# Moving six batches of the shared FFN into the scan loop, C's rows in two half buffers, and the row scaling to VectorE

## The chip, the cores and the metric

The kernel runs on one core of a Trainium2 chip. Time is the device time of one execution in microseconds (us). Before the change three runs took 1523.89, 1524.09 and 1526.13 us; the median is 1524.09.

## What is computed

x has 8 batches of 512 tokens with 256 channels, all in fp32. A layer norm, a selective scan (Mamba-like, 512 inner channels, 16 states), a residual with a norm, then a mixture of experts with a shared expert and one routed expert of eight per token:

```
h = silu(conv4(layernorm(layernorm(x)) @ in_proj_w.T))
dt_in, B, C = split(h @ x_proj_w.T);  dt = softplus(dt_in @ dt_proj_w.T + dt_proj_b)
state_t = exp(-exp(A_log) * dt_t) * state_(t-1) + B_t * h_t          # 512 x 16 values
y_t = sum_n(state_t * C_t) + D * h_t;   a = silu(y) @ out_proj_w.T + shortcut
x1 = x + layernorm(a);  xn = layernorm(x1)
shared = (silu(xn @ sh_gate) * (xn @ sh_up)) @ sh_down               # 256 -> 512 -> 256
e = argmax(xn @ gate_w);  xs = xn * sigmoid(max(xn @ gate_w))
out = x1 + layernorm(shared + (silu(xs @ rt_gate[e]) * (xs @ rt_up[e])) @ rt_down[e])
```

## The kernel before

**The scan loop.** A turn i of the loop handles the scans of batch i in 32 steps q: two halves of the 512 channels, 16 states each. At a step VectorE scans (L1067), ScalarE writes the decays of two steps ahead into PSUM (two exps, L711), and GpSimd weighs the state with C's row (L495). TensorE sums the weighed states into bank psY by 16 small matmuls in the profile (`total`, L1434). The scan's input is B's row times the channels: for even q GpSimd makes it (`inject`, L484) from rows that a DMA has spread over all partitions; for odd q TensorE spreads the row into bank psB by a matmul with a column of the identity (`spread_b`, L1426) and VectorE multiplies (L1055). In the same 32 steps run the front of batch i+1 (transposes L1340, in-projection L1350, taps L1007, dt row L1357, B and C rows L1363, softplus, dt sums L1377 to L1379) and the back of batch i-1 (out-projection L1393, norms, transposes L1407, expert logits L1416). Both share bank psF. Each engine's order is written out by the step q, and an engine runs strictly in it; a wait holds all that stands behind.

**Which waits matter here.** `spread_b` of step q+2 is issued at odd step q, after VectorE has consumed the bank at step q. `total(q-3)` waits for GpSimd's weighing. `decays(q+2)` waits for scan q. VectorE's L1030 waits for the out-projection. C's 16 rows of a batch lie in cbc, loaded once a turn in four groups of four (`load_c`), and serve both halves. SP issues nearly all loads and stores, each behind the waits before it.

**Behind the scans.** When the last batch's back is done, TensorE runs the shared FFN of all eight batches (L1490, L1512), each batch's columns xnT being loaded again from DRAM. Meanwhile VectorE works out the slots of the tokens, SP loads two batches of rows (xrow) and the routed weights (12.6 MB), GpSimd scales the rows by the score and scatters them, 4 indirect DMAs a batch (L550); the rows of batch b wait for the scatters of batch b-2. When all are scattered, SP loads slot tiles (L427), and TensorE runs 39 routed tiles (L1534, L1543, L1552, L1560). Then each token's result is gathered (L561), summed, normed and stored.

## Time and profile before

| | us |
|---|---|
| median of 3 runs | 1524.09 (1523.89 to 1526.13) |
| profiled execution | 1533.3, its span 1531.4 |
| turns 2 to 6 of the scan loop, each | 119.0 to 120.7 |
| turn 7 | 104.0 |
| shared FFN, first matmul to last | 1048.67 to 1218.4 |
| routed tiles | 1218.4 to 1466 |

The page says: TensorE busy 1204.2 us of the span, VectorE 1020.5, GpSimd 1014.7, ScalarE 799.8. A share of the whole says little here, because the stretches have different limits: GpSimd is busy nearly all of the scan loop and not at all in the routed stretch. The chain that ended last is laid on GpSimd for 36% of the span and on TensorE for 34%.

### The profile page before, as it was taken

The page shows a single profiled execution, that of the slowest core. Times are in us where ns is not written, and L with a number is a line of the kernel's source. Part 1 is how long each engine was busy: PE and PEld are TensorE (multiplying, and loading weights), DVE is VectorE, ACT ScalarE, POOL GpSimd, SP SyncE. Part 2 cuts the span into 40 slices and gives each one's busy share as a digit, 9 for nine tenths or more (in the row PEclk, how much of TensorE's full clock was granted, in tenths as well). Part 3 has the DMA queues.
Part 4 walks back from the last instruction along what each step waited for, and adds up shares of the span by engine and source line. Part 5 has one row for each costly group of instructions (what it writes and reads, how often), then busy time and mean ns, then how long its engine had stood idle before and what let it go on. Part 6 is the DMA issues. An engine that isn't in the chain of part 4 may idle for free.

```text
span 1531.4 us, 15602 instructions
## 1 busy us (share of the span) xinstructions
PE 1204.2 (79%) x4766; PEld 526.9 (34%) x4767; DVE 1020.5 (67%) x1059; ACT 799.8 (52%) x1386; POOL 1014.7 (66%) x476
## 2 busy tenths in 40 slices
PE   4774877869769878878887877757999999999920
PEld 2221223224224223223222322233655655665510
DVE  4698998998898998998998997924111022232245
ACT  6666667668658667668667664533111111111135
POOL 0599999999999999999999999931450000000043
PEclk9897899899899899899899898877999999999965
DMA  2802301401321220230230230027730111111144
GB/s 60 312 0 76 119 0 57 157 22 57 104 76 46 94 97 23 89 124 2 96 125 2 97 124 1 28 82 262 287 131 14 46 54 41 41 41 48 34 139 146
DMA packets 77953, 128.46 MB, mean 84 GB/s; under 512 B 7616, under 2 KB 56384, under 8 KB 73792
## 3 DMA queue, kind: packets, MB, share of 16 engines
q1 hardware_dynamic: 67120, 108.93, 20.6%
q10 hardware_dynamic: 7696, 10.36, 1.9%
q0 software_dynamic: 3072, 8.39, 1.7%
q8 instruction: 30, 0.49, 0.1%
q14 instruction: 35, 0.29, 0.1%
HBM read 95.94 MB, written 31.72 MB: 83 GB/s over the span
## 4 chain that ended last, share of the span: by engine, by line
POOL 36%; PE 34%; issue 13%; DVE 9%; ACT 7%; DMA 1%; another core or an unknown queue 0%; ACTq 0%; POOLq 0%; DVEq 0%
POOL state L495 22%; POOL bx L484 12%; PE psX L1543 10%; PE psX L1490 7%; DVE state L1067 4%; PE bank L1560 2%; PE psY L1560 2%; PE psY L1512 2%; PE bank L1512 2%; PE bank L1393 2%; PE psY L1434 1%; POOL lt L500 1%; DVE acc L1007 1%; ACT psX L711 1%; PE bank L1426 1%
## 5 line engine op out<-in xcount | busy, mean ns | idle before, releaser
L495 POOL TENSOR_TENSOR state<-state,cbc 128x1024 f32<-128x1024 f32 x256 | 606.4, 2391 | 12.5 <-DVE state L1067 12.4
L1067 DVE TENSOR_TENSOR_SCAN state<-psX,bx 128x1024 f32<-128x1024 f32 x256 | 578.0, 2278 | 42.9 <-ACT psX L711 23.9
L711 ACT ACTIVATE psX<-dt,aneg 128x511 f32<-128x511 f32 x512 | 330.6, 679 | 216.5 <-DVE state L1067 215.4
L484 POOL TENSOR_TENSOR bx<-xh,bbc 128x1024 f32<-128x1024 f32 x128 | 309.7, 2420 | 59.0 <-DMA bbc<-bc_rows 42.5
L1434 PE MATMUL psY<-state,ident 64*64 64x512 f32 x2048 | 303.2, 683 | 51.5 <-POOL state L495 51.3
L561 POOL DMA_INDIRECT fy<-slot_out,slot x32 | 31.9, 998 | 346.8 <-DMA slot_out<-yo 334.0
L1426 PE MATMUL bank<-prow,ident 128*128 128x512 f32 x256 | 170.2, 752 | 104.4 <-DVE bx L1055 104.2
L1055 DVE TENSOR_TENSOR bx<-xh,bank 128x1024 f32<-128x1024 f32 x128 | 152.9, 1194 | 0.5 <-PE bank L1426 0.5
L1434 PEld LDWEIGHTS psY<-state,ident 64*64 64x64 f32 x2048 | 64.8, 144 | 247.8 <-issue 123.7
L1221 DVE TENSOR_TENSOR actN<-sg,psX 128x512 f32<-128x512 f32 x39 | 26.8, 687 | 144.9 <-ACT sg L910 144.9
L1426 PEld LDWEIGHTS bank<-prow,ident 128*128 128x128 f32 x256 | 47.3, 220 | 202.2 <-DVE bx L1055 160.8
L910 ACT ACTIVATE sg<-psX 128x512 f32<-128x512 f32 x39 | 23.3, 597 | 161.6 <-PE psX L1543 161.6
L1174 DVE TENSOR_TENSOR actS<-sg,psX 128x512 f32<-128x512 f32 x32 | 21.9, 686 | 124.4 <-ACT sg L873 107.1
L1543 PE MATMUL psX<-wg,xsT 128*128 x156 | 78.8, 628 | 2.5 <-DVE xsT L1215 0.9
L1543 PE MATMUL psX<-wu,xsT 128*128 x156 | 73.9, 596 | 0.0
L1350 PE MATMUL bank<-lt,win 128*128 128x512 f32 x112 | 55.5, 618 | 20.7 <-DVE acc L1007 19.9
L1393 PE MATMUL bank<-wout,yv 128*128 128x256 f32 x256 | 61.5, 395 | 8.9 <-ACT yv L670 7.9
L873 ACT ACTIVATE sg<-psX 128x512 f32<-128x512 f32 x32 | 19.1, 597 | 92.2 <-PE psX L1490 92.2
L1007 DVE SCALAR_TENSOR_TENSOR acc<-bank,cw,acc 128x511 f32<-128x511 f32 (+2 forms) x84 | 62.3, 742 | 3.7 <-ACT acc L615 1.4
L1490 PE MATMUL psX<-xg,shg 128*128 128x512 f32 x128 | 62.1, 608 | 1.7 <-DVE actS L1174 1.7
L1490 PE MATMUL psX<-xg,shu 128*128 128x512 f32 x128 | 60.3, 593 | 0.0
L1393 PEld LDWEIGHTS bank<-wout,yv 128*128 128x128 f32 x256 | 48.7, 195 | 28.6 <-issue 12.7
(183 smaller groups left out, 1529.1 us busy)
## 6 DMA issues: line engine op xcount, KB each, us to landing
cbc<-bc_rows SPq DMA_DIRECT2D x32, 1024.0 KB, 5.1
bbc<-bc_rows SPq DMA_DIRECT2D x16, 1024.0 KB, 6.0
slot_in<-ao SPq DMA_DIRECT2D x1, 4992.0 KB, 27.3
xsl<-slot_in SPq DMA_DIRECT2D x39, 128.0 KB, 2.2
slot_out<-yo ACTq DMA_DIRECT2D x39, 128.0 KB, 2.4
xin<-in_x SPq DMA_DIRECT2D x8, 512.0 KB, 4.2
xr<-in_x SPq DMA_DIRECT2D x8, 512.0 KB, 5.8
x_rows<-ao SPq DMA_DIRECT2D x8, 512.0 KB, 2.9
```

Source lines behind the costliest of these rows:

```text
L484: nc.gpsimd.tensor_tensor(bx[q % RB][:], xh[par][:, h * CH:(h + 1) * CH], bbc[:, n // 2].unsqueeze(1).broadcast_to([P, CH, L]), ALU.mult). ...
L495: nc.gpsimd.tensor_tensor(w[:], w[:], cbc[:, n].unsqueeze(1).broadcast_to([P, CH, L]), ALU.mult).then_inc(weighted, 1)
L711: e = nc.scalar.activation(decay[q % RD][:, c, 1:L], dt[par][:, h * CH + c, 1:L], ACT.Exp, scale=aneg[:, h * CH + c, n:n + 1])
L1007: last = nc.vector.scalar_tensor_tensor(out=acc[:, c, m:L], in0=psF[:, 0:L - m], scalar=cw[:, c, TAPS - 1 - m:TAPS - m], in1=acc[:, c, m:L ...
L1055: nc.vector.tensor_tensor(bx[q % RB][:], xh[par][:, h * CH:(h + 1) * CH], psB[:].unsqueeze(1).broadcast_to([P, CH, L]), ALU.mult).then_inc ...
L1067: nc.vector.tensor_tensor_scan(st[q % RS][:].rearrange("p c t -> p (c t)"), decay[q % RD].rearrange("p c t -> p (c t)"), bx[q % RB][:].rea ...
L1393: last = nc.tensor.matmul(psF[:, (j % 2) * DIM:(j % 2 + 1) * DIM], yv[:, c, j * P:(j + 1) * P], wout[:, c], start=(c == 0), stop=(c == C - 1))
L1426: nc.tensor.matmul(psB[:], ident[:, n:n + 1].broadcast_to([P, P]), prow[par][:], start=True, stop=True).then_inc(b_bcast, 1)
L1434: done = nc.tensor.matmul(psY[o * HP:(o + 1) * HP, r], weights(half, c), src[half, c], start=first, stop=last_)
L1490: last = nc.tensor.matmul(bank, w[:, k, c * P:(c + 1) * P], xg[i][:, k], start=(k == 0), stop=(k == KC - 1))
L1512: last = nc.tensor.matmul((psF, psG)[j // 2][:, (j % 2) * DIM:(j % 2 + 1) * DIM], actS[gp][:, c, j * P:(j + 1) * P], shd[:, c], start=(c = ...
L1543: last = nc.tensor.matmul(bank, xsT[i][:, k], w[:, bass.ds(ereg[i], 1), k].rearrange("p a n -> p (a n)"), start=(k == 0), stop=(k == KC - 1))
```

## The change

**In the scan loop.** From turn 2 on, turn i also runs the shared FFN of batch i-2 (e below), whose columns xnTb are still in SBUF. It uses psB, the bank of the spread rows. At steps 1, 3, 5, 7 TensorE makes a quarter of the gate product, ScalarE copies it to `sga`, and applies Silu to all at step 10. At 13, 15, 17, 19 it makes a quarter of the up product, and VectorE multiplies it into `sga` from the bank. At 21, 23, 25, 27 it makes 128 tokens of the down product, and ScalarE copies them to `ystage`, which SP stores to DRAM. At these steps `spread_b(q+2)` is not issued; it is issued at q+1, as `spread_b(q+1)` in that step's terms, after a wait that the piece has been taken out of the bank. Other steps keep their order.

**To make room** C's rows are held in two slots of four rows, loaded in eight groups a turn. The shared weights are loaded at the start and stay.

**Behind the scans** TensorE runs the shared FFN of batches 6 and 7 only. The rows of all eight batches are loaded at once into the places of fx0 and ysh, VectorE scales them between its FFN products, and GpSimd only scatters. The stored shared rows of batches 0 to 5 (3 MB) are loaded behind x1's first half, before the third slot tile is asked for.

```diff
+    EARLY_AT = (1, 3, 5, 7, 13, 15, 17, 19, 21, 23, 25, 27)
+    CS = N // CG
+    LATE = 2
+    EARLY = NB - LATE
-        cbc = sb("cbc", [P, N, L], where=A)
+        cbc = sb("cbc", [P, 2 * CG, L], where=A)
+        sga = sb("sga", [P, FC, L], where=A)
+        ystage = sb("ystage", [P, J, DIM], where=A)
-        xrow = [sb(f"xrow{i}", [P, J, DIM], where=R) for i in range(2)]
+        xrow = [(fx0, ysh)[b // (NB // 2)][:, b % (NB // 2) * J:(b % (NB // 2) + 1) * J] for b in range(NB)]
 # SP
+            for dst, src in ((shg, sh_gate), (shu, sh_up), (shd, sh_down)):
+                sp.dma_start(dst[:], src.rearrange("(k p) n -> p k n", p=P)).then_inc(sh_loaded, 16)
+            def load_c(f, k):
+                g, slot = k % CS, k % 2
+                if not (isinstance(f, int) and f == 0 and k < 2):
+                    sp.wait_ge(weighted, Q * f + CG * (k - 1))
...
+                if do_scan and not (isinstance(i, int) and i < 2):
+                    e = i - 2
+                    sp.wait_ge(e_kept, J * (e + 1))
+                    sp.dma_start(pick(yshb_v, e), ystage[:]).then_inc(e_stored, 16)
                 if do_front:
-                    load_b(f, 1 - par, 1)
+                    load_c(f, 0)
...
-            sp.wait_ge(s_down, 2 * NB)
             load_residual(fx0, 0)
+            sp.wait_ge(e_stored, 16 * EARLY)
+            sp.dma_start(ysh[:, 0:EARLY * J, :], ysht_v[:, 0:EARLY * J, :]).then_inc(ysh_loaded, 16)
 # GpSimd
-                pool.wait_ge(xrow_loaded[b % 2], 16 * (b // 2 + 1))
-                nc.gpsimd.tensor_tensor(xrow[b % 2][:], xrow[b % 2][:],
-                                        score[:, b * J:(b + 1) * J].unsqueeze(2).broadcast_to([P, J, DIM]),
-                                        ALU.mult).then_inc(xrow_scaled, 1)
                 pool.wait_ge(xrow_scaled, b + 1)
 # ScalarE
+            def early(e, q):
+                if q in (1, 3, 5, 7):
+                    c = q // 2
+                    act.wait_ge(e_gate, FC * e + c + 1)
+                    nc.scalar.activation(sga[:, c], psB[:], ACT.Identity).then_inc(e_gate_kept, 1)
+                if q == 10:
+                    act.wait_ge(e_gate_kept, FC * (e + 1))
+                    nc.scalar.activation(sga[:], sga[:], ACT.Silu).then_inc(e_silu, 1)
+                if q in (21, 23, 25, 27):
+                    j = (q - 21) // 2
+                    act.wait_ge(e_down, J * e + j + 1)
...
+                    nc.scalar.activation(ystage[:, j], psB[:, 0:DIM], ACT.Identity).then_inc(e_kept, 1)
 # VectorE
+            def early_act(e, c):
+                dve.wait_ge(e_silu, e + 1)
+                dve.wait_ge(e_up, FC * e + c + 1)
+                nc.vector.tensor_tensor(sga[:, c], psB[:], sga[:, c], ALU.mult).then_inc(e_act, 1)
...
+                    if do_choose and q in (13, 15, 17, 19):
+                        early_act(i - 2, (q - 13) // 2)
...
+            scale_rows(0)
+            for u in range(2, LATE * FC):
+                scale_rows(u - 1)
                 sh_act(u // FC, u // FC, u % FC)
...
+            scale_rows(NB - 1)
 # TensorE
+            def early(e, q):
+                if q in (1, 3, 5, 7, 13, 15, 17, 19):
...
+                    for k in range(KC):
+                        last = nc.tensor.matmul(psB[:], w[:, k, c * P:(c + 1) * P], xnTb[:, k],
+                                                start=(k == 0), stop=(k == KC - 1))
+                    last.then_inc(e_gate if gate else e_up, 1)
+                if q in (21, 23, 25, 27):
...
+                        last = nc.tensor.matmul(psB[:, 0:DIM], sga[:, c, j * P:(j + 1) * P], shd[:, c],
+                                                start=(c == 0), stop=(c == FC - 1))
...
+            def early_taken(e, q):
+                if q in (1, 3, 5, 7):
+                    pe.wait_ge(e_gate_kept, FC * e + q // 2 + 1)
+                if q in (13, 15, 17, 19):
+                    pe.wait_ge(e_act, FC * e + (q - 13) // 2 + 1)
+                if q in (21, 23, 25, 27):
+                    pe.wait_ge(e_kept, J * e + (q - 21) // 2 + 1)
...
                 for q in range(Q):
-                    if q % 2 == 1:
+                    if do_scan and i >= 2:
+                        if q in EARLY_AT:
+                            pe.wait_ge(dve_bx, i * DQ + q // 2 + 1)
+                            early(i - 2, q)
+                        if q - 1 in EARLY_AT:
+                            early_taken(i - 2, q - 1)
+                            spread_b(i, par, q + 1)
+                    if q % 2 == 1 and not (do_scan and i >= 2 and q in EARLY_AT):
```

TensorE's order in a turn of the loop, from step 13 to the first half of the out-projection of step 15, first in the kernel before. `bank<-prow` is a spread into psB, `psY<-state` a total, `bank<-xh,w_bc` the B and C rows, `bank<-wout,yv` half of the out-projection.

```order
L1426 MATMUL bank<-prow,ident 128x512
L1434 MATMUL psY<-state,ident 64x512 x8
L1363 MATMUL bank<-xh,w_bc 128x512 x4
L1426 MATMUL bank<-prow,ident 128x512
L1434 MATMUL psY<-state,ident 64x512 x4
L1393 MATMUL bank<-wout,yv 128x256 x8
```

The same place after the change; `bank<-xnTb,shu` is an up product.

```order
L1470 MATMUL bank<-xnTb,shu 128x512 x2
L1494 MATMUL psY<-state,ident 64x512 x4
L1456 MATMUL bank<-prow,ident 128x512
L1494 MATMUL psY<-state,ident 64x512 x4
L1393 MATMUL bank<-xh,w_bc 128x512 x4
L1470 MATMUL bank<-xnTb,shu 128x512 x2
L1494 MATMUL psY<-state,ident 64x512 x4
L1423 MATMUL bank<-wout,yv 128x256 x8
L1456 MATMUL bank<-prow,ident 128x512
```

Two up products have come in, at the head of steps 13 and 15. The spread that stood at the head of step 15, ahead of the out-projection, stands behind it now.

TensorE's order at steps 25 to 28, before: L1377 to L1379 are the three matmuls that sum dt for a quarter of the channels.

```order
L1426 MATMUL bank<-prow,ident 128x512
L1434 MATMUL psY<-state,ident 64x512 x4
L1377 MATMUL bank<-acc,ident 128x512
L1378 MATMUL bank<-tmp,ident 128x512
L1379 MATMUL bank<-lt,minus 128x512
L1434 MATMUL psY<-state,ident 64x512 x4
L1377 MATMUL bank<-acc,ident 128x512
L1378 MATMUL bank<-tmp,ident 128x512
L1379 MATMUL bank<-lt,minus 128x512
L1426 MATMUL bank<-prow,ident 128x512
```

And after, from the spread of the same row on, which stood ahead of the dt sums of step 25 and stands behind them now, at step 26; `bank<-shd,sga` is a down product.

```order
L1456 MATMUL bank<-prow,ident 128x512
L1494 MATMUL psY<-state,ident 64x512 x4
L1407 MATMUL bank<-acc,ident 128x512
L1408 MATMUL bank<-tmp,ident 128x512
L1409 MATMUL bank<-lt,minus 128x512
L1477 MATMUL bank<-shd,sga 128x256 x4
L1494 MATMUL psY<-state,ident 64x512 x4
L1407 MATMUL bank<-acc,ident 128x512
L1408 MATMUL bank<-tmp,ident 128x512
L1409 MATMUL bank<-lt,minus 128x512
L1456 MATMUL bank<-prow,ident 128x512
```

The down product of step 27 stands between the dt sums of steps 26 and 27, and the last spread, which stood ahead of the dt sums of step 27, stands behind them.

ScalarE's order at the end of step 26 and at step 27, before: half an application of the norm to xr, a pair of exps, the copy of dt, the other half.

```order
L592 ACTIVATE xr<-ao,nmr,rstd 128x256 x2
L707 REGISTER_ALU
L711 ACTIVATE psX<-dt,aneg 128x511 x2
L655 ACTIVATE dt<-bank 128x512
L592 ACTIVATE xr<-ao,nmr,rstd 128x256 x2
```

And after:

```order
L610 ACTIVATE xr<-ao,nmr,rstd 128x256 x2
L740 REGISTER_ALU
L744 ACTIVATE psX<-dt,aneg 128x511 x2
L673 ACTIVATE dt<-bank 128x512
L610 ACTIVATE xr<-ao,nmr,rstd 128x256 x2
L727 ACTIVATE ystage<-bank 128x256
```

The copy out of psB (`ystage<-bank`) is the last thing of step 27.

## Rows read from the trace of the kernel before

**Rows 1.** busy time by stretch: length, busy us by engine, granted clock, DMA share, GB/s

```profile
545.50:665.60 120.10, 97.51 (x432) 34.51 (x424) 109.26 (x95) 86.25 (x143) 117.78 (x51) 0.90 0.22 78
...
903.70:1007.70 104.00, 75.87 (x347) 22.59 (x346) 85.90 (x66) 52.03 (x96) 104.00 (x46) 0.82 0.07 26
1048.67:1218.40 169.73, 167.99 (x517) 98.61 (x517) 31.23 (x64) 29.57 (x49) 47.44 (x46) 0.99 0.41 147
```

**Rows 2.** order of time, GpSimd, one turn: start us, us, what, waits

```profile
582.99 2.35 POOL L495 TENSOR_TENSOR state<-state,cbc 128x1024 f32<-128x1024 f32 x1 [0.34 <-DVE state L1067]
...
612.87 2.37 POOL L495 TENSOR_TENSOR state<-state,cbc 128x1024 f32<-128x1024 f32 x1 [1.57 <-DVE state L1067]
```

**Rows 3.** order of time, VectorE, the same turn

```profile
586.89 4.47 DVE L1067 TENSOR_TENSOR_SCAN state<-psX,bx 128x1024 f32<-128x1024 f32 x2 [0.69 <-ACT psX L711]
...
597.05 1.20 DVE L1055 TENSOR_TENSOR bx<-xh,bank 128x1024 f32<-128x1024 f32 x1
601.32 0.69 DVE L1030 TENSOR_TENSOR ao<-bank,ao 128x512 f32<-128x512 f32 x1 [3.07 <-PE bank L1393]
...
614.89 1.20 DVE L1055 TENSOR_TENSOR bx<-xh,bank 128x1024 f32<-128x1024 f32 x1
...
629.86 1.19 DVE L1055 TENSOR_TENSOR bx<-xh,bank 128x1024 f32<-128x1024 f32 x1
...
645.12 1.20 DVE L1055 TENSOR_TENSOR bx<-xh,bank 128x1024 f32<-128x1024 f32 x1
...
656.67 2.29 DVE L1067 TENSOR_TENSOR_SCAN state<-psX,bx 128x1024 f32<-128x1024 f32 x1 [1.25 <-ACT psX L711]
```

**Rows 4.** order of time, TensorE, the same turn

```profile
567.75 1.98 PE L1350 MATMUL bank<-lt,win 128*128 128x512 f32 x4 [1.69 <-DVE acc L1007]
...
579.06 2.07 PE L1426 MATMUL bank<-prow,ident 128*128 128x512 f32 x2 [5.00 <-DVE bx L1055]
...
592.05 3.70 PE L1363 MATMUL bank<-xh,w_bc 128*128 128x512 f32 x8 [0.60 <-ACT acc L626]
595.59 1.02 PE L1426 MATMUL bank<-prow,ident 128*128 128x512 f32 x2
...
597.56 3.72 PE L1393 MATMUL bank<-wout,yv 128*128 128x256 f32 x16
...
635.02 1.53 PE L1377 MATMUL bank<-acc,ident 128*128 128x512 f32 x2
```

**Rows 5.** order of time, ScalarE, the same turn

```profile
565.52 1.30 ACT L711 ACTIVATE psX<-dt,aneg 128x511 f32<-128x511 f32 x2 [1.69 <-DVE state L1067]
566.76 2.06 ACT L592 ACTIVATE ao<-xr,nmr,rstd 128x256 f32<-128x256 f32 x4
...
580.54 1.91 ACT L621 ACTIVATE xh<-acc 128x2048 f32<-128x2048 f32 x1
...
638.31 0.60 ACT L655 ACTIVATE dt<-bank 128x512 f32<-128x512 f32 x1 [1.44 <-PE bank L1379]
```

**Rows 6.** DMA issues by line: count, KB each, median us to landing

```profile
cbc<-bc_rows SPq DMA_DIRECT2D x32, 1024.0 KB, 5.1
```

**Rows 7.** order of time behind the scans: GpSimd, SP's queue

```profile
1136.60 0.96 POOL L550 DMA_INDIRECT slot_in<-xrow,slot  x1 [0.30 <-issue]
...
1139.06 0.82 SPq L427 DMA_DIRECT2D xsl<-slot_in  x2
```

**Rows 8.** groups by line, gathers and scatters: count | busy us, mean ns

```profile
L561 POOL DMA_INDIRECT fy<-slot_out,slot x32 | 31.9, 998 | 346.8 <-DMA slot_out<-yo 334.0 <-issue 9.1 <-remote 3.7
L550 POOL DMA_INDIRECT slot_in<-xrow,slot x32 | 31.3, 977 | 9.5 <-issue 7.3 <-POOL xrow L544 2.2
```

**Rows 9.** busy time by stretch while the routed weights load

```profile
1080.00:1090.00 10.00, 10.00 (x41) 7.50 (x40) 0.69 (x1) 1.79 (x3) 0.00 (x0) 1.00 1.06 401
```

**Rows 10.** order of time, TensorE, start of the routed stretch

```profile
1218.43 0.38 PE L1534 MATMUL bank<-ident,xsl 128*128 128x128 f32 x2
...
1227.35 0.66 PE L1534 MATMUL bank<-ident,xsl 128*128 128x128 f32 x2 [3.17 <-issue]
```

More of the change, by code:

```diff
@@ L151, in build @@
         actS = [sb(f"actS{i}", [P, FC, L], where=MS) for i in range(2)]
+        xg = [sb(f"xg{i}", [P, KC, L], where=MS) for i in range(2)]
         MS.close()
@@ L271, in build @@
         ex_ready = sem("ex_ready")
-        xrow_loaded = [sem(f"xrow_loaded{i}") for i in range(2)]
+        xrow_loaded = [sem(f"xrow_loaded{i}") for i in range(NB)]
         xrow_scaled = sem("xrow_scaled")
@@ L369, in iteration @@
                 if do_scan:
-                    load_c(i, par, 3)
+                    for k in range(1, 5):
+                        load_c(i, k)
                 if do_front:
@@ L1516, in sh_down_ @@
                         last.then_inc(s_down, 1)
[L1518 removed]
+            for u in range(2, LATE * FC):
                 sh_up_(u // FC, u % FC, u // FC)
             sh_down_(0, 0)
[L1521 to L1526 removed]
+            sh_down_(1, 1)
             def xsT_(s, i):
```

139 lines of the change are left out of this document (68 added, 71 removed).

## The prediction

> **What bounds the kernel now.** I read the busy times by stretch first. One turn of the scan loop (32 steps q, the scans of one batch) takes 119 to 121 us, and GpSimd is busy for 117.8 us of a turn of 120.1, VectorE for 109.3, TensorE for 97.5, ScalarE for 86.3 [rows 1]. The last turn, with no front of a next batch, takes 104.0. Then come two stretches bound by TensorE: the shared FFN (busy 168.0 of 169.7 us) and the routed one [rows 1]. So in the scans GpSimd sets the pace, but how far VectorE runs ahead of it decides what an addition elsewhere costs. GpSimd's order of time shows it: at steps 11 and 19 of a turn it starts within 0.1 us of VectorE's scan, after waits of 0.34 and 1.57 us [rows 2, 3]. The next turn's scan 0 ends at 658.96 and is weighed at 665.60 [rows 1, 3]: 6.6 us of lead, gone again by step 11. A delay of VectorE between steps 11 and 19 is therefore paid in full, and one between 20 and 31 is paid at the next step 11. VectorE waits 3.07 us at step 16 for the output projection [rows 3], and there TensorE works without a gap: from 592.05 on its rows touch until the projection's second half is done, 607.96 [rows 4]. It has idle time elsewhere (5.00 us before step 11's spread), and 0.90 is its mean granted clock in that turn [rows 1, 4].
>
> **The shared FFN among the scans (six turns, 2 to 7).** Each turn gains 12 pieces in bank psB: 4 gate products at steps 1 to 7, 4 up products at 13 to 19, 4 down products at 21 to 27. A gate or up product is shaped like the in-projection (1.98 us as a row, 1.82 from its start to the next one's), a down product is half of an L1393 row of 3.65, so 1.8: 12 x 1.8 = 22 us for TensorE. VectorE gains 4 products like the additions of 0.69 us, of which 0.62 counts back to back: 2.5 us. ScalarE gains 4 copies of 0.60, 4 of half that size, and one Silu of 1.91 [rows 3 to 5]. That alone would fit. What does not fit is the bank: the spread of row q+2 was issued two steps ahead; now it waits at step q+1 until the piece has been taken out, and who takes it out is an engine in order. I walk through the turn, "late" meaning against the rows.
>
> Gates. After scan q ScalarE does two exps (1.30), then the copy (0.60), then TensorE spreads (1.1): 3.0 us, while VectorE needs 2.2 for scan q+1. At 3, 5 and 7 the three taps (2.2) cover this, but at 5 and 7 ScalarE has moments or a 2.06 us application ahead of the copy: together 1.2 us late. At step 1 the gate product stands ahead of the transposes of the next front, and their copy ahead of its own: 2.3 us. Sum 3.6 [rows 4, 5].
>
> Ups. The Silu at step 10 stands ahead of exps 13, for which VectorE already waits (0.69 before 586.89): 1.8 late at scan 13. The row of L1363 starts 1.9 late, at 593.9, since z comes later. Behind it now stand an up product and a total before the projection, which ends at 604.0 where 601.2 was. The spread for step 17, which stood ahead of the projection (595.59), now stands behind it: inject 17 at 605.05 where it was 597.05, scan 17 at 606.9 where it was 601.9 (601.32 and the 0.61 of the addition), some 4.9 late. The next up product and again a spread behind the projection give scan 19 6.9 late, and inject 21 at 622.6 for 614.89: 7.7 late [rows 3, 4].
>
> Downs. At 21 the copy waits behind an application: 1.7, of which the end of VectorE's wait for GpSimd's `loss` gives back nearly all. At 23 it stands behind Relu and half an application: inject 25 at 640.0 for 629.86, 10.1 late. From step 25 to 28 TensorE has no gap (in the old turn its rows touch from 635.02 on), so the pieces of 25 and 27 lengthen it by 3.6, and the piece of 27 leaves the bank only after the copy of dt, which follows its three matmuls, and half an application (1.0): inject 29 at 661.9 for 645.12, 16.7 late. VectorE's old waits for ScalarE there (the longer is 1.25, before 656.67) give back 1.4: 15.3 at the next scan 0. If the wait of 4.6 us before the spread of 25 lets the clock fall to its lower level, as 5.00 us of idle did before 579.06 (the spread took 2.07 there instead of 1.1), 1.2 to 2 more [rows 3 to 5].
>
> A turn grows by 3.6 + 15.3 + 1.7 = 20.6 us; five turns (2 to 6) by 103. The ends are far apart: VectorE's 2.5 us and its present waits alone give 5, all 22 us of TensorE with the bank's round trips 28. I take 20.6, the walk, since the waits it adds hang on rows with names. In turn 7 there is no front: VectorE needs 112 for its walk with twelve waits of 0.8 where GpSimd needs 104 after a start 9.9 us behind: 114 against 113.9 from scan 0 on, nothing.
>
> **C's rows by halves.** Eight loads a turn for four, 5.1 us each from issue to landing [rows 6]; a load is let go when its slot's group is done and is wanted four steps (14 us) later. SP issues in order, and ahead of group 0 of the next turn stand the stores of xn and of the shared rows, which wait for ScalarE's step 27; that leaves some 9 us. I take 0, with GpSimd's own waits as the cover; if it goes, up to 5 us a turn. The three shared weights are loaded at the start behind wout, 1.5 MB in an idle queue: 0.
>
> **The stretch behind the scans.** Six of eight batches leave the shared FFN, so TensorE is free at about 1097. Then the scatter is the end of the wait. Before, GpSimd scattered batches 0 and 1 at once, then waited for its rows behind the routed weights, and scaled each batch itself; the last of 32 went at 1136.60 and SP asked for the first slots at 1139.06 [rows 7]. Now all rows are in place and VectorE scales. VectorE's first scaling comes behind its routing (1066.2), so the first scatter is 1 us later, at 1067.5; then 32 x (0.98 + 0.30) = 41 us [rows 8], the last at 1107, slots asked for at 1109.6. The weights saturate the queues at 401 GB/s [rows 9], 17 MB from 1049 with 3 MB more rows ahead of them: in at about 1101, not the end. The first slot transpose, at 1218.43 before [rows 10], comes at 1112. There a wait grows: the third slot load stood behind 2 MB of x1 (TensorE waits 3.17 us, until 1227.35 [rows 10]); now also behind 3 MB of stored shared rows, 8 us at the same rate: until 1127.5. Gain 1227.35 - 1127.5 = 99.9, less 1 to 2 for a clock that falls in the longer wait: 98. Bounds: 92 if the scatter's landings lag, 104 if the 3 MB are quick. The 39 routed tiles and the end are unchanged.
>
> Here a rule can be weighed. VectorE now scales with both inputs in SBUF while GpSimd issues scatters. In the trace 32 gathers with VectorE's additions beside them took a mean of 998 ns, 32 scatters without them 977 [rows 8]: 0.7 us in all, which the sum leaves out. The Trainium skill (SBUF — State Buffer, Who interferes with whom) says that a VectorE instruction with two SBUF inputs takes the read port that GpSimd shares and holds it for the whole instruction, and infers that descriptor writing is spared. By the hold alone eight scalings would cost up to 8 x 1.2 = 10 us; by the inference nothing, and the trace agrees with the inference.
>
> **Sum.** 103 + 0 - 98 = +5. The profiled execution took 1533.3 us (span 1531.4); the median of the runs is 1524.1, so I put +6 on it, rounding up for clock falls: 1530.
>
> **Rivals.** (1) The waits overlap: VectorE, once late, finds ScalarE's and TensorE's queues empty, and a turn grows by 12 only. For it speaks that TensorE idles 22 us a turn [rows 1]; against it that the additions sit where it does not. 5 x 12 - 98 = -38: 1486. Chance 0.27. (2) GpSimd stays the bound, the lead of 6.6 us takes the additions, a turn grows by 3: 15 - 98: 1441. Against it rows 2: no lead at steps 11 to 19. 0.08. (3) The lower clock level meets the pieces too, in the stretches behind each new wait: a turn grows by 26: 1558. 0.15. (4) C's halves come late, 5 us a turn on top: 1555 and above, deciding once a load takes over 14 us from its release. 0.05. (5) The forecast, a turn of 136 to 145: 0.45.
>
> **How the numbers follow.** A measurement of this kernel tells 0.2%, 3 us, from no change. The forecast's case spreads 15 us to each side: of its 0.45, 0.28 is slower, 0.10 the same, 0.07 faster. Faster: 0.27 + 0.08 + 0.07 = 0.42; same 0.10; slower 0.28 + 0.15 + 0.05 = 0.48. The forecast's own range is 1512 to 1550. The range for 8 in 10 takes in most of rivals 1, 3 and 4 and leaves out rival 2: 1482 to 1560.
>
> **What would show it.** In the profile after: turns of 136 to 145 us by the distance of GpSimd's first weighings; GpSimd busy about 85% of one, waiting for the scan; VectorE's inject waiting for the bank, most at steps 17, 19, 25 and 29; the first slot transpose some 106 us earlier relative to the last weighing than the 210.7 us of before, and about 10 us of idle TensorE before the third. Turns under 130 us, or GpSimd waits put down to a DMA of cbc, would prove the walk wrong.

## The result, and the profile after

The changed kernel took 1541.6 us (median of 4 runs, 1539.33 to 1541.9) where the kernel before took 1525.07 in the same series (4 runs, 1523.89 to 1526.13): a ratio of 1.0105 (1.0088 to 1.0123). In a second series it was 1542.64 against 1522.46, 1.0126 (1.0105 to 1.0148). So it is slower by 1.1 to 1.3%, 16 us in the first series and 20 in the second, where 6 were forecast. The profiled execution took 1541.9 us, its span 1540.2.

I cut both spans at the same places of the work (us; the scans' and weighings' starts and ends, TensorE's third slot transpose, the first gather):

| stretch | before | after | difference | forecast |
|---|---|---|---|---|
| scan 0 of turn 2 to scan 0 of turn 7 | 596.5 | 706.7 | +110.2 | +103 |
| scan 0 of turn 7 to the last weighing's end | 113.9 | 120.7 | +6.8 | 0 |
| from there to the third slot transpose | 219.7 | 122.2 | -97.5 | -98 |
| routed tiles, up to the first gather | 244.2 | 240.7 | -3.5 | 0 |
| first gather to the end of the span | 59.8 | 52.6 | -7.2 | 0 |

Ahead of the first row both take 297 us. The last row is most likely not the change's: the experiment before_again and its neighbours speak for that below. Without it the sum is +16, which is what the ratio of the first series says.

Busy time by stretch, after: a turn of the loop twice, then the last weighings of turn 7.

```profile
440.10:582.10 142.00, 116.29 (x488) 44.73 (x488) 114.19 (x100) 92.77 (x154) 118.32 (x51) 0.95 0.29 100
582.10:725.30 143.20, 119.52 (x488) 46.06 (x488) 113.68 (x99) 91.12 (x151) 118.21 (x50) 0.93 0.28 96
1007.10:1124.70 117.60, 91.13 (x430) 33.77 (x430) 95.25 (x74) 60.78 (x111) 106.62 (x46) 0.94 0.23 87
```

GpSimd's work in a turn is what it was (118.2 us against 117.78 [rows 1]), but the turn is 22 us longer, so its share falls to 83% (118.21 of 143.2): it is no longer the bound. No other engine is the new one either: TensorE is busy for 119.5 of 143.2, VectorE for 113.7. What fills the turn are waits, and the costliest groups and the chain of waits of the page say whose:

```profile
PE 47%; DVE 18%; ACT 16%; issue 9%; POOL 7%; DMA 1%; ACTq 0%; DVEq 0%; POOLq 0%; SPq 0%
...
L518 POOL TENSOR_TENSOR state<-state,cbc 128x1024 f32<-128x1024 f32 x256 | 606.7, 2384 | 67.1 <-DVE state L1088 66.6
...
L1456 PE MATMUL bank<-prow,ident 128*128 128x512 f32 x256 | 157.3, 699 | 147.2 <-DVE bx L1076 57.5
L1076 DVE TENSOR_TENSOR bx<-xh,bank 128x1024 f32<-128x1024 f32 x128 | 154.3, 1205 | 117.1 <-PE bank L1456 117.0
```

GpSimd was 36% of the chain and is 7%. It waits 66.6 us for VectorE's scans (L1088) before its weighings and another 74.9 before its own injects (L506). VectorE's inject (L1076) waits 117.0 us for the spread (L1456): in turns 3 to 6 these waits of VectorE are 33 and take 79.1 us, where the kernel before had none. The spread in turn is held by the piece that is in the bank.

### The profile page after: what moved, and what is told of

It is laid out like the page before. It is cut to its first block, busy times and chain, and to the rows that moved or that the text cites. A ratio compares the mean times of both kernels' runs of the same rounds, so it can differ in the third digit from the quotient of the medians.

```text
span 1540.2 us, 15716 instructions
## 1 busy us (share of the span) xinstructions
PE 1199.0 (78%) x4766; PEld 518.9 (34%) x4767; DVE 1036.7 (67%) x1067; ACT 812.1 (53%) x1404; POOL 1007.4 (65%) x468
## 4 chain that ended last, share of the span: by engine, by line
PE 47%; DVE 18%; ACT 16%; issue 9%; POOL 7%; DMA 1%; ACTq 0%; DVEq 0%; POOLq 0%; SPq 0%
DVE state L1088 10%; PE psX L1604 10%; PE psY L1494 6%; PE bank L1456 5%; ACT psX L744 4%; PE bank L1423 4%; DVE bx L1076 3%; PE bank L1470 3%; PE bank L1621 2%; PE bank L1380 2%; POOL slot_in L568 2%; PE psY L1621 2%; PE bank L1407 2%; POOL state L518 2%; POOL fy L579 2%
## 5 line engine op out<-in xcount | busy, mean ns | idle before, releaser
L518 POOL TENSOR_TENSOR state<-state,cbc 128x1024 f32<-128x1024 f32 x256 | 606.7, 2384 | 67.1 <-DVE state L1088 66.6
L1088 DVE TENSOR_TENSOR_SCAN state<-psX,bx 128x1024 f32<-128x1024 f32 x256 | 579.3, 2279 | 41.1 <-ACT psX L744 25.1
L506 POOL TENSOR_TENSOR bx<-xh,bbc 128x1024 f32<-128x1024 f32 x128 | 308.6, 2411 | 118.0 <-DVE state L1088 74.9
L1494 PE MATMUL psY<-state,ident 64*64 64x512 f32 x2048 | 295.9, 662 | 11.0 <-POOL state L518 11.0
L1456 PE MATMUL bank<-prow,ident 128*128 128x512 f32 x256 | 157.3, 699 | 147.2 <-DVE bx L1076 57.5
L1076 DVE TENSOR_TENSOR bx<-xh,bank 128x1024 f32<-128x1024 f32 x128 | 154.3, 1205 | 117.1 <-PE bank L1456 117.0
L1494 PEld LDWEIGHTS psY<-state,ident 64*64 64x64 f32 x2048 | 61.1, 139 | 197.2 <-issue 149.9
L926 ACT ACTIVATE sg<-psX 128x512 f32<-128x512 f32 x39 | 23.3, 597 | 184.7 <-PE psX L1604 184.7
L1456 PEld LDWEIGHTS bank<-prow,ident 128*128 128x128 f32 x256 | 43.8, 203 | 227.4 <-DVE bx L1076 79.8
L1023 DVE SCALAR_TENSOR_TENSOR acc<-bank,cw,acc 128x511 f32<-128x511 f32 (+2 forms) x84 | 62.5, 745 | 7.6 <-ACT acc L633 5.4
L1244 DVE COPY xsT<-bank 128x256 f32<-128x256 f32 x39 | 16.5, 424 | 62.4 <-PE bank L1595 62.4
L1477 PE MATMUL bank<-shd,sga 128*128 128x256 f32 x192 | 52.1, 418 | 7.5 <-DVE bx L1076 7.5
L1470 PE MATMUL bank<-xnTb,shu 128*128 128x512 f32 x96 | 48.5, 629 | 7.3 <-DVE bx L1076 7.3
L1470 PE MATMUL bank<-xnTb,shg 128*128 128x512 f32 x96 | 49.3, 639 | 2.1 <-DVE bx L1076 2.1
```

Of the source, the lines that this page charges most:

```text
L506: nc.gpsimd.tensor_tensor(bx[q % RB][:], xh[par][:, h * CH:(h + 1) * CH], bbc[:, n // 2].unsqueeze(1).broadcast_to([P, CH, L]), ALU.mult). ...
L518: nc.gpsimd.tensor_tensor(w[:], w[:], cbc[:, n % (2 * CG)].unsqueeze(1).broadcast_to([P, CH, L]), ALU.mult).then_inc(weighted, 1)
L1076: nc.vector.tensor_tensor(bx[q % RB][:], xh[par][:, h * CH:(h + 1) * CH], psB[:].unsqueeze(1).broadcast_to([P, CH, L]), ALU.mult).then_inc ...
L1088: nc.vector.tensor_tensor_scan(st[q % RS][:].rearrange("p c t -> p (c t)"), decay[q % RD].rearrange("p c t -> p (c t)"), bx[q % RB][:].rea ...
L1456: nc.tensor.matmul(psB[:], ident[:, n:n + 1].broadcast_to([P, P]), prow[par][:], start=True, stop=True).then_inc(b_bcast, 1)
L1470: last = nc.tensor.matmul(psB[:], w[:, k, c * P:(c + 1) * P], xnTb[:, k], start=(k == 0), stop=(k == KC - 1))
```

## How a turn grew

VectorE's waits for the spread in turn 4 that are longer than 1.7 us. Scan 0 of the turn starts at 579.42 (before at 537.2, so that 42.2 is to be added to the times of [rows 2 to 5] to compare):

```profile
590.71 1.22 DVE L1076 TENSOR_TENSOR bx<-xh,bank 128x1024 f32<-128x1024 f32 x1 [3.21 <-PE bank L1456]
...
653.42 1.22 DVE L1076 TENSOR_TENSOR bx<-xh,bank 128x1024 f32<-128x1024 f32 x1 [2.64 <-PE bank L1456]
...
662.25 1.22 DVE L1076 TENSOR_TENSOR bx<-xh,bank 128x1024 f32<-128x1024 f32 x1 [2.03 <-PE bank L1456]
...
688.90 1.22 DVE L1076 TENSOR_TENSOR bx<-xh,bank 128x1024 f32<-128x1024 f32 x1 [3.19 <-PE bank L1456]
...
712.19 1.22 DVE L1076 TENSOR_TENSOR bx<-xh,bank 128x1024 f32<-128x1024 f32 x1 [6.48 <-PE bank L1456]
```

These are the injects of steps 3, 17, 19, 25 and 29: the four that the prediction named, and step 3, to which it gave less. (At step 23 it waits 1.65 us, at 7 and 9 some 0.3.) TensorE at steps 15 to 17 and 24 to 29; a total (L1494) is 8 small matmuls in the profile, not 16:

```profile
645.98 1.88 PE L1470 MATMUL bank<-xnTb,shu 128*128 128x512 f32 x4
647.79 1.09 PE L1494 MATMUL psY<-state,ident 64*64 64x512 f32 x8
648.81 3.72 PE L1423 MATMUL bank<-wout,yv 128*128 128x256 f32 x16
652.37 1.02 PE L1456 MATMUL bank<-prow,ident 128*128 128x512 f32 x2
...
686.79 2.08 PE L1456 MATMUL bank<-prow,ident 128*128 128x512 f32 x2 [4.20 <-ACT ystage L727]
688.79 1.99 PE L1494 MATMUL psY<-state,ident 64*64 64x512 f32 x8
690.71 3.19 PE L1477 MATMUL bank<-shd,sga 128*128 128x256 f32 x8
...
711.03 1.12 PE L1456 MATMUL bank<-prow,ident 128*128 128x512 f32 x2 [1.93 <-ACT ystage L727]
```

Up product, total, projection and only then the spread: the rows touch, as forecast, and inject 17 starts at 653.42. At step 24 the spread waits 4.20 us for ScalarE's copy and then takes 2.08 us, the total behind it 1.99 for 1.09: after that idle time these rows and most of the down product behind them (3.19 for 1.99) are at the lower of the two clock levels (the granted clock from 687 to 693 is 0.50). They are 3.1 us longer together, of which the spread's 1.0 is on VectorE's path at once; the prediction had 1.2 to 2. Why the copy is late stands in ScalarE's order:

```profile
682.35 1.30 ACT L744 ACTIVATE psX<-dt,aneg 128x511 f32<-128x511 f32 x2 [0.30 <-DVE state L1088]
683.59 1.89 ACT L669 ACTIVATE acc<-acc 128x2048 f32<-128x2048 f32 x1
685.39 1.04 ACT L610 ACTIVATE bank<-ao,nmr,rstd 128x256 f32<-128x256 f32 x2
686.37 0.36 ACT L727 ACTIVATE ystage<-bank 128x256 f32<-128x256 f32 x1
```

A copy of 0.36 us stands behind Relu (L669) and half an application of the norm (L610), 2.8 us together. That nobody is in a hurry for these two is what copy_first shows below.

How late each point of turn 4 is against before, counted from scan 0 of the turn (us, from the starts of VectorE's scans and injects), beside the forecast and two kernels from the experiments:

| | forecast | after | copy_first | ups_moved |
|---|---|---|---|---|
| scan 11 | 3.6 | 5.7 | 1.4 | 1.4 |
| scan 13 | 5.4 | 7.5 | 3.2 | 3.2 |
| scan 17 | 8.5 | 11.0 | 6.1 | 3.2 |
| scan 19 | 10.5 | 13.1 | 8.2 | 3.2 |
| inject 21 | 11.3 | 13.7 | 8.7 | 4.0 |
| inject 25 | 13.7 | 16.8 | 8.6 | 3.7 |
| inject 29 | 20.3 | 24.8 | 12.1 | 5.5 |
| scan 31 | | 24.0 | 11.3 | 11.3 |

The forecast's column is 3.6 plus the prediction's own 1.8, 4.9, 6.9, 7.7, 10.1 and 16.7.

Behind the scans, first TensorE's first and third slot transposes, then the first, one slow and the last scatter of GpSimd, then SP's queue (the x1 loads stand just ahead of these rows):

```profile
1230.59 0.66 PE L1595 MATMUL bank<-ident,xsl 128*128 128x128 f32 x2 [17.21 <-DMA xsl<-slot_in]
...
1246.88 0.66 PE L1595 MATMUL bank<-ident,xsl 128*128 128x128 f32 x2 [8.81 <-issue]
```

```profile
1183.00 1.20 POOL L568 DMA_INDIRECT slot_in<-fx,slot  x1 [16.70 <-DVE fx L1230]
...
1194.17 1.86 POOL L568 DMA_INDIRECT slot_in<-fx,slot  x1 [0.30 <-issue]
...
1226.11 0.97 POOL L568 DMA_INDIRECT slot_in<-ysh,slot  x1 [0.30 <-issue]
```

```profile
1231.53 0.95 SPq L460 DMA_DIRECT2D ysh<-shared_rows  x1
1232.86 23.76 SPq L448 DMA_DIRECT2D xsl<-slot_in  x4
```

The first transpose comes 105.9 us after the last weighing (210.7 before, [rows 10]; 106 sooner were forecast, it is 104.8). The scatters run from 1183.00 to 1226.11, 43.1 us where 41 were reckoned. The third slot load is asked for behind 2 MB of x1 and 3 MB of shared rows, and TensorE waits 8.81 us before the third transpose; 10 were forecast. The row names no reason for this wait ("issue"); that it is the load's shows in slots_first below.

## Experiments

The first four kernels ran on one chip, where the kernel before had a median of 1530.05 us (7 runs, 1528.77 to 1534.51). The second four ran on another (1524.04, 1522.8 to 1525.32), the last three on a third (1522.46, 9 runs, 1520.26 to 1525.11).

### before_again: the kernel before, unchanged

> The kernel before, profiled once more. From the third slot transpose to the end of the span the profile of before has 304.1 us and that of the changed kernel 293.3, with nothing changed there but the place of a load. Theory: the 8 us by which the profiled execution of before (1533.3) lies over its median (1525.1) sit in this stretch and are an accident of that execution: now the span is 1523 to 1525 and the stretch 294 to 297. Rival: the change really shortens the stretch: again 302 to 305 with a span near 1531.

One execution: 1533.4 us, span 1531.7. From the third slot transpose to the end it took 304.4 us, as the first profile of before (304.1), where the changed kernel takes 293.3. So the long end was no chance of a single run, and the expectation that it was one is wrong. ScalarE, GpSimd and VectorE in it, among the gathers:

```profile
1504.83 1.09 ACT L952 ACTIVATE fy<-fy,fnm,frs 128x256 f32<-128x256 f32 x2 [2.32 <-issue]
1505.76 0.94 POOL L561 DMA_INDIRECT fy<-slot_out,slot  x1 [1.70 <-issue]
1506.92 0.75 DVE L1256 BATCH_NORM_STATS2 fst<-fy 128x6 f32<-128x256 f32 x2 [5.59 <-remote]
```

Three engines stand still within the same few us, and no instruction of the program is named as what they wait for. VectorE's pause of 5.59 us has a twin of 4.95 eight us earlier, in which ScalarE stands still too but GpSimd does not. Such pauses are in five profiles, the first one of the kernel before and the four of the first series, and in none of the other eight. The group of the same line in copy_first (first series) and in the changed kernel:

```profile
L1287 DVE BATCH_NORM_STATS2 fst<-fy 128x6 f32<-128x256 f32 x32 | 12.0, 418 | 10.9 <-remote 5.6 <-issue 4.2 <-DVE fy L1284 0.7
```

```profile
L1285 DVE BATCH_NORM_STATS2 fst<-fy 128x6 f32<-128x256 f32 x32 | 12.0, 418 | 0.5
```

From the first gather to the end these five take 59.1 to 61.3 us, the other eight 52.3 to 52.9. Kernels with the change's tail are on both sides, so for them it goes with the series and not with the kernel. The kernel before has no profile without pauses; that it runs without them elsewhere follows from times alone (a median of 1524.04 and 1522.46 us on the two later chips, 1530.05 on the first series' one). So the 7.2 us of the table's last row are most likely none of the change's, and most of the 9 us by which the first profile of before lies above its own runs' median are these pauses. What they are stays open; nothing in the program was varied to find out.

### none_early: no piece of the shared FFN in the scan loop

```diff
-    EARLY_AT = (1, 3, 5, 7, 13, 15, 17, 19, 21, 23, 25, 27)
+    EARLY_AT = ()
```

With it the copies, the Silu, the products and the stores of the pieces are left out; C's half buffers, the tail and the 3 MB load stay. The shared results of batches 0 to 5 are missing from the output.

> Leaves out the shared FFN of batches 0 to 5 altogether (the rows of x1 are loaded in its place); C's rows by halves, VectorE's scaling and the short shared stretch stay. Theory: the stretch behind the scans gains 97.5 and C's halves cost nothing, so turns of 119 to 120.5 and 1427 us (1422 to 1433). Rival, C's halves or the eight loads cost the loop: turns of 122 to 125, GpSimd waiting for a DMA of cbc, 1440 to 1460.

1432.43 us (1431.68 to 1436.92), ratio 0.9361 (0.9336 to 0.9387). Turns 2 to 5 take 119.3 to 119.6 us, as before (119.5 to 120.1). GpSimd over four turns:

```profile
440.00:904.00 464.00, 375.09 (x1640) 133.16 (x1636) 421.58 (x360) 331.53 (x542) 457.33 (x191) 0.90 0.32 110
```

It is busy for 457.3 of 464 us. Eight loads of C's rows for four cost nothing, and the whole 110 us are the pieces'. The expectation is met. Without them the change would gain 6.4%.

### copy_first: ScalarE takes the gate and down pieces out before its other work of the step

```diff
                         decays(i + 1, 1 - par, q + RD - Q)
+                    if do_early and q != 10:
+                        early(i - 2, q)
                     if do_back and q == SUM_LAG - 1:
...
-                    if do_early:
+                    if do_early and q == 10:
                         early(i - 2, q)
```

> ScalarE takes a gate or down piece out of the bank right behind the exps of its step, ahead of the front's and back's work of that step. Theory (the cost is the bank's round trip behind an engine in order): the copies of steps 1, 5, 7, 21, 23 and 27 come 0.5 to 2.5 us sooner, a turn shrinks by 5 to 8 us, from 141.5 to 134 to 136: 1505 to 1518. Rival (the cost is TensorE's 22 us of added work in a turn): turns stay at 140 to 142 and the time at 1538 to 1543.

1485.41 us (1482.4 to 1489.06), ratio 0.9704 (0.9676 to 0.9732). Not one instruction was added or taken away, and turns 2 to 6 went from 140.2 to 142.7 down to 128.8 to 130.3; I had expected 134 to 136. The mean granted clock in turn 4 is 0.97, where it is 0.93 in the changed kernel, so a part of the gain may be the clock's; no run separates the two. VectorE's waits for the spread from step 20 to 31 of turn 4 are two, before injects 23 and 29 (none before 25, where it was 3.19), and then ScalarE at step 25:

```profile
649.25 1.22 DVE L1078 TENSOR_TENSOR bx<-xh,bank 128x1024 f32<-128x1024 f32 x1 [0.67 <-PE bank L1458]
...
676.29 1.22 DVE L1078 TENSOR_TENSOR bx<-xh,bank 128x1024 f32<-128x1024 f32 x1 [3.36 <-PE bank L1458]
```

```profile
663.30 1.30 ACT L744 ACTIVATE psX<-dt,aneg 128x511 f32<-128x511 f32 x2 [3.86 <-DVE state L1090]
664.54 0.36 ACT L727 ACTIVATE ystage<-bank 128x256 f32<-128x256 f32 x1
```

The copy follows the exps; from inject 21 to inject 29 the turn loses 3.4 us more instead of 11.1 (the table). The gates lose 1.4 us instead of 5.7. That leaves the ups, 1.4 to 8.7, whose pieces VectorE takes out.

### slots_first: slot tiles asked for ahead of the shared rows and x1

```diff
-            load_residual(fx0, 0)
-            sp.wait_ge(e_stored, 16 * EARLY)
-            sp.dma_start(ysh[:, 0:EARLY * J, :], ysht_v[:, 0:EARLY * J, :]).then_inc(ysh_loaded, 16)
+            for s in range(4):
+                sp.wait_ge(xsT_ready, s + 1)
+                load_slots(s + 2, s % 2)
+                if s:
...
+                    sp.dma_start(ysh[:, half, :], ysht_v[:, half, :]).then_inc(ysh_loaded, 16)
```

> SP loads the slot tiles of the first steps first, and the stored shared rows and the first half of x1 in parts behind slot loads 2 to 8. Theory (the third slot load stands behind 5 MB): TensorE's 8.8 us wait before the third slot transpose goes, and some of the lower clock behind it: 1530 to 1534. Rival (the parts then hold up later slot loads as much): 1538 to 1543.

1540.58 us (1539.46 to 1545.33), ratio 1.0071 (1.0045 to 1.0097), against 1.0105 and 1.0126 for the change: some 5 us, though the third slot transpose comes 113.6 us after the last weighing instead of 122.2, with no wait ahead of it any more. The interval overlaps the first of the change's two, so this run alone leaves the gain unsure. The time is in the rival's range; as a ratio to a before of 1525 the theory's range is 1.003 to 1.006 and the rival's 1.009 to 1.012, and the result lies between. With the copy moved as well (below) the same edit is clearly measured.

### half_products: half of the matmuls of each piece left out

```diff
-                    for k in range(KC):
+                    for k in range(1):
...
-                    for c in range(FC):
+                    for c in range(FC // 2):
```

Each gate and up product sums one half of the channels, each down product two of four blocks; waits and copies stay.

> The changed kernel with half of the matmuls of every piece in the scan loop (one of the two channel halves of gate and up, two of four quarters of down), so the shared rows of batches 0 to 5 are not the reference's. All takings out of the bank stay. Theory (round trips and places): only what stands on the late paths shrinks, one half product at step 1, at 13, 15, 17, 19, 25 and 27, 0.9 each: turns of 134 to 137 instead of 141.5. Rival (TensorE's added time as such): 11 us less a turn, 129 to 132.

One execution: 1537.81 us. Turns 2 to 6 took 138.8 to 142.4 us, 140.6 on average where the whole pieces give 141.3. Both expectations missed: 11 us less of matmuls a turn (twelve pieces, 0.9 each at the full clock) bought 0.7. Its busy time in the stretch of turn 4, and TensorE's spread of step 24 with the down product behind it:

```profile
582.10:725.30 143.20, 114.13 (x466) 40.35 (x470) 115.45 (x101) 93.11 (x154) 120.96 (x51) 0.90 0.29 98
```

```profile
683.90 2.08 PE L1456 MATMUL bank<-prow,ident 128*128 128x512 f32 x2 [5.06 <-ACT ystage L727]
687.83 2.07 PE L1477 MATMUL bank<-shd,sga 128*128 128x256 f32 x4
```

Before step 24 TensorE now waits 5.06 us for the same copy where it waited 4.20. The halved product behind it is wholly at the lower clock level and takes 2.07 us, as long as a whole one at the full clock (1.99); in the changed kernel the whole one there took 3.19. The mean granted clock of the stretch fell from 0.93 to 0.90, and TensorE's busy time by 5.4 us only.

Most of what the shorter products bought was spent again at another place. Over turns 3 to 6 VectorE's injects wait 69.5 us for the spread where they waited 79.1. But VectorE's taps (L1023) now wait 11.3 us for the in-projection and the copy behind it where they waited 4.4. In turn 4 the reason is in the rows: TensorE's spread of step 6 waits 4.12 us for ScalarE's copy and takes 1.87 us for 1.12, and the total behind it, ahead of the in-projection, is at the lower level too. So this run shows that shorter products alone hardly pay here: TensorE waits longer and its clock falls. It does not separate their length from the clock: what half the length would be worth at an unchanged clock no run here shows.

### ups_moved: copy_first, with up products at 13, 19, 21, 23 and the down products in two pairs

```diff
+    EARLY_AT = (1, 3, 5, 7, 13, 19, 21, 23, 25, 29)
+    UPS = (13, 19, 21, 23)
+    DOWNS = (25, 29)
```

> With ScalarE's copies first, and the same products at other steps: the up products of steps 15 and 17, which stand ahead of the out-projection, move to 21 and 23, and the four down products are done in pairs at 25 and 29, one copy for two; the spreads at 15 and 17 stand where they stood. Theory (the place ahead of the out-projection costs): of the 8.1 us that scan 19 is late, 5 go, steps 20 to 31 add 1 or 2: turns of 124 to 127 where 129.3 are now, 1458 to 1472. Rival (the added work costs wherever it stands): turns of 128 to 131 and 1480 to 1492.

1468.01 us (1467.49 to 1471.11), ratio 0.9639 (0.9623 to 0.9655). Up to inject 29 it did what was expected: with no piece at steps 15 and 17 the spreads stand ahead of the projection again, and scans 17 and 19 are 3.2 late instead of 6.1 and 8.2. But from inject 29 to scan 31 it gives 5.8 of it back, and turn 4 takes 129.4 us for 129.9. The gain in time comes from turns 5 to 7 (127.4, 126.0 and 111.7 for 128.9, 128.8 and 114.4) and from the pauses that this series does not have.

### copy_and_slots and all_three

copy_and_slots is copy_first with the edit of slots_first, all_three is ups_moved with that edit.

> ScalarE's copies first, and the first slot tiles loaded ahead of the shared rows. Theory: both effects add, 8 us less than copies first alone, 1475 to 1480 against a before of 1530. Rival (the loads in parts hold up later slots, or the end gives the gain back): 1483 to 1488.

1470.3 us (1468.35 to 1471.52), ratio 0.9643 (0.9627 to 0.966). The range expected, 1475 to 1480, was against a before of 1530, which is a ratio of 0.964 to 0.967: as a ratio it is met. Its turns are copy_first's (128.8 to 131.3). Of the 15 us between it and copy_first some 9 are the pauses of the first series (302.1 and 293.1 us from the third slot transpose to the end).

> Copies first, up products moved off the out-projection, slot tiles first. Theory: turns as in ups_moved (124 to 127) and 8 us less behind the scans: 1450 to 1464. Rival: no better than copy_and_slots, 1475 to 1488.

1460.88 us (1459.53 to 1462.45), ratio 0.9584 (0.9568 to 0.96), as expected, and against ups_moved of the same series 7.1 us less: that is the worth of slots_first where nothing disturbs it. In turn 4 the second pair of down products (3.62 us of TensorE, from 676.36) holds VectorE, here before the inject of step 31:

```profile
682.49 1.22 DVE L1090 TENSOR_TENSOR bx<-xh,bank 128x1024 f32<-128x1024 f32 x1 [4.63 <-PE bank L1470]
```

### downs_27: all_three with the second pair at step 27

```diff
-    DOWNS = (25, 29)
+    DOWNS = (25, 27)
```

> As all_three, but the second pair of down products at step 27 instead of 29. In ups_moved a scan is 3.8 to 6.5 us late up to step 29 and 4.7 more at step 31, where the spread waits for the copy of that pair behind ScalarE's and TensorE's work of steps 29 and 30. Theory (the place of the taking out decides): at 27 the pair costs 1 to 3, turns of 124.5 to 127 where 128.4 are now: 1440 to 1455. Rival (3.6 us of TensorE between the dt sums cost more than at 29): turns of 128 to 131 and 1460 to 1475.

1461.82 us (1458.88 to 1462.88), ratio 0.9603 (0.959 to 0.9616): no gain. The range expected was missed, and the rival's was met in the time; the turns are 126.7 to 129.4 us. The wait has moved one inject earlier and is longer:

```profile
674.61 1.22 DVE L1090 TENSOR_TENSOR bx<-xh,bank 128x1024 f32<-128x1024 f32 x1 [6.01 <-PE bank L1470]
```

```profile
666.30 3.62 PE L1491 MATMUL bank<-shd,sga 128*128 128x256 f32 x16
...
673.55 1.02 PE L1470 MATMUL bank<-prow,ident 128*128 128x512 f32 x2
```

Between these two rows stand a total and three dt sums, without a gap: 8.3 us from the pair's start to the spread's end. Here TensorE's own time counts, as it does ahead of the projection. A pair costs VectorE 6 us here (5.4 to 11.5 late) and 5.8 at step 29.

### short_scale: seven of VectorE's eight scalings cut to one column

```diff
+                part = slice(0, DIM) if b < 1 else slice(0, 1)
```

Only batch 0's rows are scaled whole; the others' scatters carry unscaled rows.

> The changed kernel, in which VectorE scales only one of 256 columns of the rows of batches 1 to 7 (the scattered rows are not the reference's), so no long VectorE instruction with two inputs in SBUF runs beside the scatters. In the changed kernel six of 32 scatter issues beside such scalings took 1.20 to 1.86 us where the rest took 0.97. Theory (they hold GpSimd up): all but one or two issues take 0.97 and the 32 end 3 to 4 us sooner after the first, 39.6 instead of 43.1 us. Rival (queue or loads in flight hold them up): again 5 or 6 issues of 1.2 to 1.9 us.

One execution, 1537.32 us. GpSimd's scatters out of the first buffer, first of the changed kernel, then of this one:

```profile
L568 POOL DMA_INDIRECT slot_in<-fx,slot x16 | 19.1, 1196 | 21.3 <-DVE fx L1230 16.7 <-issue 4.6
L568 POOL DMA_INDIRECT slot_in<-ysh,slot x16 | 15.5, 968 | 4.9 <-issue 4.9
```

```profile
L568 POOL DMA_INDIRECT slot_in<-fx,slot x16 | 15.7, 981 | 21.3 <-DVE fx L1231 16.7 <-issue 4.0 <-DVE ysh L1231 0.6
```

1196 ns a scatter fall to 981, and the last of 32 goes at 1222.75 instead of 1226.11. All but the first (1.17 us) take 0.97. The scalings of 1.2 us cost the scatters beside them 3.4 us, as expected.

### changed_again: the changed kernel once more, on the third chip

> The changed kernel once more beside the others on one chip. From its profile: turns of 140 to 143 and a time 0.9 to 1.2% over before. The stretch from the third slot transpose to the end was 293.3 us in its first profile and 299 to 302 in the profiles of the variants: theory, that it was an accident, now 299 to 304; rival, 293 again.

1542.64 us (1538.62 to 1544.79), ratio 1.0126 (1.0105 to 1.0148). Its stretch from the third slot transpose to the end is 292.1 us without a pause, as in the first profile of it (293.3). So the expectation that the short end was an accident is wrong too, and the series is left as what differs among kernels with the change's tail. Turn 7 is 122.8 us here, 2.1 more than in the first profile; the difference arises behind step 13, and its reason is open.

## Why the prediction was right, and where it was off

**The mechanism was right.** The pieces' cost is the bank's way from engine to engine in their written orders, with VectorE late and GpSimd behind it. The turns lie in the forecast's 136 to 145 (140.2 to 142.7 by the scans, 136.8 to 143.2 by GpSimd's first weighings), GpSimd is busy for 83% of one, and the waits stand at the injects it named. The point, 1530, was 11.6 us too low, and the change costs nearly three times the 6 us forecast; the wide range, 1482 to 1560, holds both.

**The turn: 20.6 was forecast, 22.0 measured.** Most of the difference is the gates: at scan 11 turns 2 to 6 are 4.4 to 6.6 us late, 5.4 in the mean, not 3.6. The rows say what the walk left out: a lower clock at the gates. The start of turn 4, then the same gate product of turn 5, and in turn 4 the spread of step 6, what stands behind it, and the taps ahead of scan 8:

```profile
583.06 2.73 PE L1470 MATMUL bank<-xnTb,shg 128*128 128x512 f32 x4
585.72 1.88 PE L1494 MATMUL psY<-state,ident 64*64 64x512 f32 x8
...
726.24 1.88 PE L1470 MATMUL bank<-xnTb,shg 128*128 128x512 f32 x4
```

```profile
606.39 1.12 PE L1456 MATMUL bank<-prow,ident 128*128 128x512 f32 x2 [2.46 <-ACT sga L718]
607.44 1.64 PE L1494 MATMUL psY<-state,ident 64*64 64x512 f32 x8
609.01 3.08 PE L1380 MATMUL bank<-lt,win 128*128 128x512 f32 x4
...
612.85 2.32 DVE L1023 SCALAR_TENSOR_TENSOR acc<-bank,cw,acc 128x511 f32<-128x511 f32 x3 [1.60 <-ACT acc L633]
```

The first gate product takes 2.73 to 2.96 us in turns 2, 4 and 6 and 1.88 in turns 3 and 5; scan 3 is 3.3 to 4.0 us late in the former and 2.2 in the latter, where I had 2.3. The granted clock from 584 to 587 is 0.50. (The kernel before is at the lower level here too, its spread at 541.74 taking 1.91 us for 1.02, but nothing of VectorE's hangs on that.) The third in-projection of turn 4, at 609.01, takes 3.08 us for 1.98 (granted clock 0.50 from 608 to 611), its result reaches ScalarE late, and VectorE's taps wait 1.60 us; in the other turns this wait is 0.57 to 1.0. In turns 3 and 5 the gates lose 4.4 and 4.6 us, of which such a wait is 1.0 and 0.8; the rest is the 3.6 of the walk. So the gates' round trips were sized right, and what the clock adds to them, by these rows an estimated 1 to 3 us a turn, was put at nothing. For the spread of step 24 the prediction did price it, at 1.2 to 2: that must be the 1.7 in its sum. From there on to inject 21 the walk held within 1 us in turn 4: 5.3, 7.4 and 8.0 over the gates at scans 17, 19 and inject 21, where 4.9, 6.9 and 7.7 were forecast. At inject 29 it is 19.1 over the gates where I had 16.7, without the clock's 1.7. Five turns make 7.2 of the 11 us by which the sum, +5, was too low.

**Turn 7: 0 was forecast, 6.8 measured.** I let twelve waits of 0.8 us pass, 9.6 in all. The inject's waits for the spread alone are nine, 17 us together, up to 2.85 before inject 9, since without a front the exps, the copy and the spread are longer than VectorE's own work of a step. That VectorE, not GpSimd, would set this turn was right; its walk was mis-sized. These 6.8 us and the turns' 7.2 make 14; the routed tiles give 3.5 of them back, which no term had.

**Behind the scans: 98 forecast, 97.5 measured,** its parts included (106 less to the first slot forecast, 104.8 measured, then 7.3 lost to the third). That it is so near is partly luck: the scatters took 2 us more than reckoned, for a reason that the prediction had ruled out (below).

**The size of the forecast itself.** The sum was +5, and I put +6 on the median of the runs, not on the profile's 1533.3. That was right, though I did not know why: most of what the profile has above the median are pauses in its last 60 us, which no term of the sum touches.

**The rivals.** Waits that overlap to +12 a turn: wrong here, but copy_first's turns (+10 on before) are near it: that took another order of ScalarE's work. GpSimd stays the bound: wrong, and its reason, no lead at steps 11 to 19, held. A lower clock: wrong as a whole, since the mean over a turn rose from 0.90 to 0.93 to 0.95; but it does meet work that now holds VectorE: the gate product of step 1, the in-projection behind the spread of step 6, and the rows from the spread of step 24 on. (By its own terms this rival gives 5 x 26 - 98 = +32, 1556, not 1558.) C's halves late: wrong by none_early.

**What was wrong in kind** is the weighing of VectorE's scalings against GpSimd's scatters. I took 0.7 us and said that the trace agrees with sparing. short_scale shows 3.4 us, with scatters of up to 1.86 us for 0.97. The gathers that I compared have a mean of 998 ns, but it hides four of 1.29 to 1.34 us among 28 of 0.94 to 1.03: the four began while an addition was running, and each ended 0.8 us after that addition. The rows say how it works: the scaling that starts at 1193.97 ends at 1195.19, and the scatter that starts beside it at 1194.17 ends at 1196.03, 0.84 us later, nearly as if it had begun only then; the one at 1190.32 (0.97 us), begun before a scaling of 1190.54, is not held. The Trainium skill (SBUF — State Buffer, Who interferes with whom) has both halves: that a VectorE instruction with two inputs in SBUF holds the shared read port, and the inference that descriptor writing is spared. These runs fit the first for the issue of an indirect DMA, and speak against counting such an issue as spared; whether it is the writing of descriptors that is held, or the reading of the slot indices, was not tried. The bound of 10 us by a full hold was too high: one of eight scalings was over before the first scatter and the second 0.15 us after its start (and the first scatter takes 1.17 us in short_scale too), three cost 0.9 us each, two 0.3 and 0.5, and one next to nothing.

What stays open: the 3.5 us that the routed tiles take less (244.2 and 243.1 before, 239.4 to 241.2 in eleven profiles with the change's tail), and the pauses.

## What to carry to other kernels

Work put into another engine's gaps costs first of all by its handovers: moving copies of 0.36 to 0.60 us ahead of 1 to 3 us of unhurried work bought 12 us a turn, half the matmuls alone bought 0.7, with a lower clock. Where a piece stands ahead of another long job, as before the projection, its length counts too. And look at the clock behind each new wait: what shorter work saves can come back as slower rows. So list, for each piece, what stands in the written order ahead of the instruction that gives the shared bank back, on every engine it passes, and move that one first; then keep pieces off the steps where another long job shares the queue. And before a few us of difference between two profiles are explained, look at engines that stand still together with nothing named as their reason: that part may go with the series of runs.

The best version is all_three: 0.9584 (0.9568 to 0.96) of the kernel before, and 5% under the changed kernel (1460.88 against 1541.6).
